# Second attention: 16 consecutive queries in a group, some far keys by one-hot products instead of gathers

## The reference

```python
I = jnp.where(local, inf, I)                    # the last 64 keys are always kept
I = jnp.where(causal, -inf, I)
_, idx = jax.lax.top_k(I, 96)                   # so 32 far keys are picked by the index scores
key_c = (c_kv @ W_uk)[bi, idx]; value = (c_kv @ W_uv)[bi, idx]
key_r = _pope((x @ W_kr)[bi, idx], angles_k)    # turned by the place in the list, not in the text
scores = (einsum(q_c, key_c) + einsum(q_r, key_r)) * scale
out = einsum(softmax(scores), value).reshape(B, L, H * D) @ W_out
```

## Time and profile before

| | us |
|---|---|
| median of 3 runs | 2763.94 |
| lowest, highest | 2754.53, 2770.24 |
| span of the profiled execution | 2263.8 |
| what lies around that span, by the median | 500.1 |
| second attention in the span, first row maximum to last output | 1598.3 to 2216.7 |

### The profile page before, as it was taken

How to read it: one execution, slowest core, us unless ns; L and a number is a source line. 1 busy time by engine, 2 the same in 40 slices (tenths; PEclk the granted TensorE clock), 3 DMA queues, 4 the chain that set the end, 5 groups by cost and what they waited for, 6 DMA issues and landing times. The chain is left out here.

```text
span 2263.8 us, 56900 instructions
## 1 busy us (share of the span) xinstructions
PE 2100.6 (93%) x22674; PEld 1263.2 (56%) x22674; DVE 1789.1 (79%) x3457; ACT 1732.0 (77%) x3507; POOL 1828.5 (81%) x1239
## 2 busy tenths in 40 slices
PE   5899999999999999999999989986999899988878
PEld 1466666666666666666666646652454444444444
DVE  7788888888888888888888658978868986887214
ACT  5798898998989988988989945657566775775543
POOL 4899999999999999999999945627777777777720
PEclk9999999999999999999999989978579996999878
DMA  4000000000000000000000000111211111111101
GB/s 153 1 2 2 2 2 2 2 2 2 2 2 2 2 2 2 2 2 2 2 2 2 2 15 23 39 39 27 52 38 32 38 33 38 31 38 36 39 10 37
DMA packets 44688, 43.19 MB, mean 19 GB/s; under 512 B 21312, under 2 KB 33424, under 8 KB 44176
## 3 DMA queue, kind: packets, MB, share of 16 engines
q1 hardware_dynamic: 28560, 23.35, 3.6%
q0 software_dynamic: 15872, 16.28, 3.1%
HBM read 33.83 MB, written 1.57 MB: 16 GB/s over the span
## 5 line engine op out<-in xcount | busy, mean ns | idle before, releaser
L380 POOL TENSOR_TENSOR probs_lo<-probs,probs_hi 128x1024 f16<-128x1024 f32 x512 | 1076.7, 2129 | 43.0 <-ACT probs L430 42.6
L494 DVE TENSOR_REDUCE part_max<-aux 128x1 f32<-128x512 f32 x1024 | 677.9, 687 | 91.0 <-PE aux L568 86.7
L429 ACT ACTIVATE probs_hi<-scores 128x512 f16<-128x512 f32 x1024 | 630.2, 615 | 134.6 <-PE scores L601 117.3
L430 ACT ACTIVATE probs<-scores 128x512 f32<-128x512 f32 x1024 | 636.6, 622 | 0.0
L1622 POOL DMA_INDIRECT far<-key_table,placeT x456 | 451.9, 991 | 142.9 <-issue 138.7
L617 PE MATMUL acc<-v,probs_hi 128*128 128x65 f16 x4096 | 451.1, 193 | 2.3 <-POOL probs_lo L380 2.3
L619 PE MATMUL acc<-v,probs_hi 128*128 128x64 f16 x4096 | 452.3, 195 | 0.0
L621 PE MATMUL acc<-v,probs_lo 128*128 128x65 f16 x4096 | 450.6, 192 | 0.0
L617 PEld LDWEIGHTS acc<-v,probs_hi 128*128 128x128 f16 x4096 | 382.5, 96 | 82.6 <-POOL probs_lo L380 2.5
L619 PEld LDWEIGHTS acc<-v,probs_hi 128*128 128x128 f16 x4096 | 380.0, 97 | 75.5
L568 PE MATMUL aux<-k_a,q_a 128*128 128x512 f16 x1024 | 392.1, 383 | 5.2 <-DVE roped L480 2.1
(11 more groups left out here) (329 smaller groups left out, 3935.5 us busy)
## 6 DMA issues: line engine op xcount, KB each, us to landing
far<-key_table,placeT POOLq DMA_INDIRECT x496, 2.4
qT<-qT SPq DMA_DIRECT2D x16, 256.0 KB, 2.9
e_w<-in_e_w SPq DMA_DIRECT2D x48, 64.0 KB, 1.9
x<-in_x SPq DMA_DIRECT2D x4, 256.0 KB, 3.9
cos<-in_cos SPq DMA_DIRECT2D x1, 1024.0 KB, 6.8
sin<-in_sin SPq DMA_DIRECT2D x1, 1024.0 KB, 8.9
e_w<-in_e_w SPq DMA_DIRECT2D x2, 512.0 KB, 3.9
out<-x SPq DMA_DIRECT2D x4, 256.0 KB, 2.7
```

The source lines that it names most:

```text
L380: pool.tensor_tensor(probs_lo[:, slot], probs[:, wide], probs_hi[:, slot], ALU.subtract).then_inc(low_ready, 1)
L429: act.activation(probs_hi[:, slot, i], bank, ACT.Exp, scale=float(DH0) ** -0.5)
L430: act.activation(probs[:, wide, i], bank, ACT.Exp, scale=float(DH0) ** -0.5).then_inc(probs_ready, 1)
L494: dve.tensor_reduce(part_max[g % 2][:, n % QT, n // QT:n // QT + 1], bank, AX.X, ALU.max).then_inc(aux_free, 1)
```

## The change

Six things are changed together, with the waits that belong to them.

1. A group of 16 queries is now 16 consecutive ones, so its near keys are a window of WIN = 96 columns (`window(t, g)`) instead of 256. A row of scores has 224 columns instead of 384. One mask serves all tiles but the first; the second mask load goes.
2. The near values of each group come by DMA from the table to `near_value` (8 DMAs of 96 rows for each tile on SP), because a window no longer starts at a multiple of 128. `sums` does 8 products of 128 columns for them, in place of 4 of 512.
3. Probabilities are transposed in 4 turns instead of 6; the context is copied by ACT in one copy for each half instead of four. The copies of the queries have another order.
4. Of the gathered keys of tiles 3 to 15, 16 columns (tiles 3 to 9) or 4 columns (tiles 10 to 15) are no longer gathered. Their places go as f16 to DRAM (`spread_places`, SP) and come back to all partitions (`placeB`). DVE compares them with the numbers of the keys (`hot`), t+1 instructions of 128x512 for each unit of 4 columns; PE multiplies these one-hot tiles with the keys split into a high and a low f16 part (`make_keys`, 8 products of 64 columns for each); ACT copies the unit to `far` (`make`). One-hot tiles lie in a ring of 4, later 8, in `qi`.
5. `ki_lo` has 128 partitions, and its product uses all of them.
6. The index queries are stored in a permuted order, so that ranks come out in the order of the new groups; tile 0 needs no extra copies of its places any more.

```diff
-WIN = 2 * P
+WIN = KTS
+def window(t, g):
+    return max(t * P + GROUP * (g + 1) - WIN, 0)
+PER = 4
+UNITS = {t: 4 if t < 10 else 1 for t in range(3, NT)}
+MADE = sorted(UNITS)
+MADE_AT = 3 - NG
+SPLIT = MADE[-1] + 1
...
-    sums = {2: [("p", c, 0)], 3: [("p", c, 2), ("p", c, 4)], 4: [("ctx", c, 0)], 6: [("p", c, 1), ("p", c, 3)],
-            7: [("p", c, 5), ("ctx", c, 1)]}
+    sums = {2: [("p", c, 0)], 3: [("p", c, 2)], 4: [("ctx", c, 0)], 6: [("p", c, 1)], 7: [("p", c, 3), ("ctx", c, 1)]}
...
+    made = j - 1 - MADE_AT
+    work += [("make", made // NG, made % NG)] if made % NG < UNITS.get(made // NG, 0) else []
     work += group("max", j - 2) + group("exp", j - 3)
...
+    t = (j - MADE_AT) // NG
+    work += [("hot", t, (j - MADE_AT) % NG)] if (j - MADE_AT) % NG < UNITS.get(t, 0) else []
...
-    return [(t, i) for t in range(NT) for i in range(gathers(t))]
+    return [(t, i) for t in range(NT) for i in range(gathers(t) - made(t))]
...
+        def ring_of(t):
+            return NIDX * (2 if t > MADE[0] else 1)
...
+                def spread_places(t):
+                    n, b = MADE.index(t), P // 32
+                    out = dram["places"][n:n + 1, 0:made(t) * P]
+                    sp.wait_ge(place16_ready, n + 1)
+                    for k in range(b):
+                        sp.dma_start(out[0].rearrange("(i b r) -> b i r", i=made(t), b=b)[k],
+                                     place16[n % PLACES][32 * (k + 1) - made(t):32 * (k + 1), :]).then_inc(place_out, 16)
+                    sp.wait_ge(place_out, (n + 1) * b * 16)
+                    if n == 0:
+                        sp.wait_ge(turn_free, free_no["q", 2, 3])
+                    else:
+                        sp.wait_ge(hot_ready, hot_no[t, 0, 0] - 1)
+                    sp.dma_start(placeB[:, 0:made(t) * P], out.broadcast_to([P, made(t) * P])).then_inc(placeB_in, 16)
...
+                    if t >= 2:
+                        sp.wait_ge(ctx_full, 2 * (t - 1))
+                    for g in range(NG):
+                        sp.dma_start(value[t % 2][:, g, :], keep["table"][window(t, g):window(t, g) + WIN, 0:CKV]
+                                     ).then_inc(value_in, 16)
+                    if t + 1 in UNITS:
+                        spread_places(t + 1)
...
+                    elif kind == "make":
+                        if i == 0:
+                            if t >= RING:
+                                act.wait_ge(ctx_full, 2 * (t - RING + 1))
+                        first = FAR - made(t) + PER * i
+                        ins = act.activation(far[t % RING][:, first:first + PER, :],
+                                             src[:, 0:PER * KW].rearrange("p (i k) -> p i k", i=PER), ACT.Copy)
...
+                def hot(t, k):
+                    if k == 0:
+                        dve.wait_ge(placeB_in, 16 * (MADE.index(t) + 1))
+                        dve.wait_ge(idx_full, idx_no["idx", ring_of(t) - 1, len(index_chunks(ring_of(t) - 1)) * NIDX - 1])
+                    for kt in range(t + 1):
+                        o = hot_no[t, k, kt] - hot_no[t, 0, 0]
+                        if o >= ring_of(t):
+                            wait_used(dve, *hots[hot_no[t, k, kt] - 1 - ring_of(t)])
+                        elif o == 0 and t > MADE[0]:
+                            wait_used(dve, *hots[hot_no[t, 0, 0] - 2])
+                        dve.tensor_scalar(hot_tile(t, k, kt), placeB[:, k * CH:(k + 1) * CH], key_id[:, kt:kt + 1], None,
+                                          ALU.is_equal).then_inc(hot_ready, 1)
...
+                def make_keys(b, t, k):
+                    if k == 0:
+                        pe.wait_ge(split_ready, 1)
+                    for kt in range(t + 1):
+                        pe.wait_ge(hot_ready, hot_no[t, k, kt])
+                        for part in range(2):
+                            for i in range(PER):
+                                ins = pe.matmul(b[:, i * KW:(i + 1) * KW], hot_tile(t, k, kt)[:, i * P:(i + 1) * P],
+                                                split[:, kt, part * KW:(part + 1) * KW], start=(kt + part + i == 0),
+                                                stop=(kt == t and part == 1), skip_group_check=True)
+                        if kt < t:
+                            ins.then_inc(hot_used, 1)
+                    return ins
...
-                    parts = [1] if t == 0 else [0, 1]
-                    for part in parts:
-                        pe.matmul(out, rows[:, t - 1 + part, 0:CKV],
-                                  probsT[:, part, HALF * c:HALF * c + HALF, :].rearrange("p g l -> p (g l)"),
-                                  start=(part == parts[0]), stop=False, skip_group_check=True)
+                    for j in range(HALF):
+                        g = HALF * c + j
+                        pe.matmul(ctxp[:, j * P:(j + 1) * P], value[t % 2][:, g, :], probsT[0:WIN, 0, g, :],
+                                  start=(j == 0), stop=False, skip_group_check=True)
...
-                        pe.matmul(out, qi[0:DH1, h, queries], ki_lo[:, lo:hi], start=False, stop=True
+                        pe.matmul(out, qi[:, h, queries], ki_lo[:, lo:hi], start=False, stop=True
                                   ).then_inc(idx_full, 1)
```

More of the change, by code:

```diff
@@ L1317, in first_rank @@
                             own.link(dve.match_replace(values, first_top[:], values, -3.4e38))
[L1318 to L1332, removed]
+                    dve.transpose(placeT[t][:], first_place[:]).then_inc(place_ready, 1)
                 for n, (kind, i) in enumerate(jobs):
@@ L1526, in gathers, with made, place_of @@
     return 32 if t else 16
+def made(t):
+    return PER * UNITS.get(t, 0)
 def gather_list():
-    return [(t, i) for t in range(NT) for i in range(gathers(t))]
+    return [(t, i) for t in range(NT) for i in range(gathers(t) - made(t))]
+def place_of(placeT, t, i):
+    column = FAR - gathers(t) + i
+    return placeT[t % PLACES][:, column:column + 1]
 def landed(t, half):
-    return 256 * (t // RING + (0 if t % RING == 0 and half else 1))
+    each = lambda s: 16 if not half else 16 - made(s) if s else 0
+    return 16 * sum(each(s) for s in range(t % RING, t + 1, RING))
 def keys_no(t, half):
@@ L1555, in selected_attention @@
             keep[n] for n in ("rows", "queries", "near_keys", "nout", "ctxT", "qi", "ki_hi", "ki_lo", "mask"))
+        value = [sb(f"near_value{i}", [WIN, NG, CKV], F32) for i in range(2)]
         space, ahead = keep["space"], keep["ahead"]
@@ L1661, in _ @@
                 for kind, t, i in schedule:
+                    if (kind, t, i) == SPLIT_AFTER:
+                        act.wait_ge(turn_full, turn_no["q", 1, 3])
+                        act.activation(split[:, :, 0:KW], rows[:, 0:SPLIT, :], ACT.Copy).then_inc(high_ready, 1)
                     if kind in TURNS and kind != "y":
@@ L2202, in tables @@
     t["cap0"] = np.where(k <= l - LW, 3.4e38, np.where(k <= l, -3.3e38, -1e36 * (k + 1))).astype(f32)
[L2204 to L2213 removed]
+    block = (row % 32 // H1)[:, None, None]
+    l = (4 * (row // 32))[:, None, None] + block + GROUP * np.arange(NG + 1)[None, :, None]
+    s = np.array([window(0, g) for g in range(NG)] + [P + GROUP - WIN])[None, :, None] + np.arange(WIN)[None, None, :]
+    first = (l < LW) & (np.arange(NG + 1) < NG)[None, :, None]
+    near = np.where(first, (s >= 0) & (s < KTS), (s > l - LW) & (s <= l))
+    far = (np.arange(P)[None, None, :] // FAR == block) & ~first
+    t["mask"] = bfloat16(np.where(np.concatenate([near, far], 2), 0.0, -1e30))
     t["unit"] = bfloat16(np.eye(P))
+    t["key_id"] = (P * np.arange(SPLIT)[None, :] + np.arange(P)[:, None]).astype(f32)
     t["iota"] = np.tile(np.arange(E0, dtype=f32), (P, 1))
@@ L2282 @@
     dram["out"] = nc.dram_tensor("out_0", (T, D), F32, kind="ExternalOutput").ap()
+    dram["places"] = nc.dram_tensor("places", (len(MADE), P * max(made(t) for t in MADE)), F16, kind="Internal").ap()
     dram["key_table"] = nc.dram_tensor("key_table", (T, KW), F32, kind="Internal").ap()
```

132 lines of the change are left out of this document (78 added, 54 removed).

## The result

The changed kernel takes 2631.35 us (2615.09 to 2644.51, 4 runs) beside 2767.09 for the kernel before (2754.53 to 2772.1, 4 runs): a ratio of 0.950, 95% interval 0.945 to 0.9545. It is faster by 136 us.

The account below looks back on a forecast made before the run. Gathers on POOL were taken to set the end only in tiles 13 to 15, PE with DVE close behind before. Window changes of -13, +8, -2 and -24 made -31 on 2763.94: 2733, range 2690 to 2785.

Parts of the forecast that it names:

- the second sentence: Timed median 2763.94 against a span of 2263.8: the 500.1 us around the profiled span were held fixed.
- A: Second attention, tiles 0 and 1, 79.7 us before: forecast 67, or -13.
- B: Second attention, tiles 2 to 8, 267.5 us before: forecast 275.6, +8, with DVE 96% busy.
- C: Second attention, tiles 9 to 12, 137.1 us before: forecast 135, -2, with DVE at 97%.
- D: Second attention, tiles 13 to 15 with the tail, 134.1 us before: forecast 110, -24, no gathers to wait for.
- the ring and the hand-over: Tiles 2 to 8: DVE and PE waiting for each other over one-hot tiles, priced at a few per cent of DVE's time.
- The sign that I had named for it: Tiles 2 to 8: DVE idle over 10%, waiting for one-hot tiles' use, would show the ring as the limit.
- rival 1: Second attention: DVE kept full and PE at full clock, -69 in all, 2695; chance 0.15.
- rivals 2, 4 and 5: DVE compares at 0.40 each, chance 0.12; far dearer at 0.67, chance 0.06; held up by gathers, chance 0.04.
- rival 5: DVE compares wait for the rest of a POOL gather, 0.25 in the mean: +61, 2794; chance 0.04.
- The low index keys: PE's index products: with 128 rows in both, 0.10 us gone twice in each of 136 pairs, 2.0 a tile.
- Rival 3, the clock: TensorE's clock falls, 0.65 in tiles 2 to 8: +44 on the forecast, 2777; chance 0.14.

Follow-up runs that it names:

- e9: Changed kernel, all far keys of tiles 3 to 14 gathered as before: 2670.0 us, long, ratio 0.9685 to the kernel before.
- e1: The changed kernel with no edit, for a second trace: 2261.35 us, short, ratio 0.998 to the kernel before.
- e13: The changed kernel with no edit, again: 2262.65 us, short, ratio 0.998 to the kernel before.
- e18: Changed kernel with two units made in tiles 3 to 9, one after: 2219.01 us, short, ratio 0.980 to the kernel before.
- e14: Changed kernel with pauses of POOL, five fills each, between gathers: 2307.79 us, short, ratio 1.019 to the kernel before.
- e3: Changed kernel with the low index keys' product on 64 rows again: 2282.44 us, short, ratio 1.008 to the kernel before.
- e2: Changed kernel, all far keys gathered as before but one unit of tile 15: 2255.33 us, short, ratio 0.996 to the kernel before.

## Why the prediction was wrong, and where it was right

**The step that failed** is the second sentence: "so 500.1 us lie around the profiled span; I hold them fixed". The spans of long executions are within 2 us of their times, and the changed kernel's long trace shows 336 of its 365 us inside the second attention, where PE, ACT and DVE stand during runs of gathers. The change removes gathers and work beside them, and so the time was not fixed: 490 to 504 us before, 356 to 370 after. Taken from the same two kinds of execution, the short gain is 4 us and the long one 136; the other 132 come from the term that I had set at zero. All the working stood on a profile of another kind of execution than the runs it was to forecast, and a gap of 18% between the two should have had rivals and a width of its own; the range of 2690 to 2785 had neither.

For the changed kernel this is shown directly. For the kernel before it is not: each of its traces is short. That its 500 us lie in the same place is inferred from the times of kernels that share its gathers. Why the chips differ stays open, and so does what stops the engines during gathers, and whether pauses of POOL would help: they were not tried on a chip with long executions. The account of the 85 us by the turns above is argued from e9's windows, not isolated by a run for each part.

**The sum, against a short execution.** It forecast -31, where -4 (e1) and -2 (e13) were measured. By windows: A 66.3 (I had 67), B 299.0 (275.6), C 141.9 (135), D 114.2 (110). The work in B was right, DVE 261.1 busy (264.6). The mis-sized term is its share: 87% busy instead of 96, the ring and the hand-over priced at a few per cent and costing 23 us. The sign that I had named for it came: DVE idle over 10% in B. The waits above say how: PE waits 32.2 us for compares, DVE 12.0 for one-hot tiles to be used and 11.0 and 9.7 for products and rectified scores behind them. DVE (87% busy) and PE (81%) waited for each other in turn; a share of 96% held for neither. One term of rival 1 does not come out as written: C at 100% is 121.8 - 5.4 + 12.5 + 0.6 = 129.5, so -8 and not -10; nothing hangs on it. With half the compares (e18) the share is 91%.

**The compares** were right, and rivals 2, 4 and 5 with their dearer prices are out. The row of the short trace (count, busy, mean ns), and its least, median and greatest ns:

```profile
L1852 DVE TENSOR_SCALAR qi<-queries,key_id 128x512 f16<-128x512 f16 x277 | 80.0, 358 | 23.5 <-PE a_turn L1931 23.5
...
L1852 DVE TENSOR_SCALAR qi<-queries,key_id x277: 311/344/571, 1670.6 to 2149.7; 128x512 f16<-128x512 f16 x139
```

80.0/277 = 0.29 each (I had 0.28) and 358 ns long (0.33 to 0.36). Gathers hold them up only a little: those that start in the first 0.47 us of a gather take their 0.34, but most that start later in it are over 0.11 to 0.12 us after the gather's end, 25 of the 277 at 0.39 to 0.57, which makes 4 us in all where rival 5 had 61. The gathers are not longer for it (977 ns in the mean beside a compare, 1024 otherwise). By the Trainium skill's rule of the shared port pair (SBUF — State Buffer, Who interferes with whom), of a DVE instruction in a two-port mode and one of GpSimd the second is blocked until the first is over. A compare that starts early in a gather is not, so for gathers the rule holds here at most for their second half; beside the fills of e14, with compares of up to 1.97 us, it holds in full.

**The low index keys** were right: 0.10 twice a pair, 21 us at the end (e3). Undoing this part alone costs more than the whole change gains in a short execution (4 us).

**Gathers and D.** POOL has idle time that waits for contexts, as said, and D fell from 134.1 to 114.2; DVE's waits for key DMAs of the earlier trace rows are gone there. That gathers set the end only in D was right for a short execution, and wrong for a long one, where every tile with a run of gathers is longer than in the short one. In the windows of e2 they set C too, once all keys are gathered.

**Rival 3, the clock.** In a short execution the clock of B is 0.90 (0.89 before): it did not fall. In the long one it is 0.74, under the 0.75 from which I had said it decides; there it goes with PE standing still in the runs (0.56 to 0.70 in those shown above, 0.76 to 0.84 between them), and the time is less than before all the same.

## What to carry to other kernels

Before a sum is built on a profile, ask whether the profiled execution is of the kind that is timed: if its span is far from the median, the difference is a term to be located, not a constant, and anything the change removes may be its cause. When two kinds of work exclude each other (here, in a long execution, a run of gathers and nearly all of the other engines' work), a stage lasts their sum, and work that was hidden becomes worth its full time on either side. When a change moves work onto an engine that is next in line, size it by where the two balance: with half of the compares the kernel was 42 us faster in a short execution than with all of them. And before a queue that runs dry is called the cause, ask who empties it: here the packets of instructions were fewer because PE used fewer.

## What the runs showed of the hardware

On some chips PE, ACT and DVE nearly stand while POOL issues indirect DMAs. In the long trace 2105 of PE's products and loads start in 380 us of gathers, in the short one, with the same program, 8080 in 408. PE goes on for some 85 products (83 to 89 in nine of e9's eleven runs of 32 gathers), and after that stands, or issues single ones at distances of 0.70 us and its multiples (2328.88, 2329.61, 2331.02 above); it is back at its pace 2 to 9 us after the end of each of the 13 runs of the long trace. Between chips this makes 356 to 504 us for 360 to 496 gathers, while DVE's and ACT's busy times hardly change (488.1 and 488.7, 347.3 and 344.2 in the second attention).

An f16 compare of 128x512 on DVE lasts 0.34 us alone and up to 1.97 beside fills of 1.8 us on POOL; beside an indirect DMA of 0.94 us it is held up only when it starts 0.49 us or more into it, by up to 0.23.
